# A graph-attention layer: gathers that skip the slots behind a group's last edge, with indices made by the vector engine

## The reference, cut to what matters

```python
q = (x @ Wq.T + bq); k = (x @ Wk.T + bk); v = (x @ Wv.T + bv)      # per node, 8 heads of 32
e = edge_attr @ We.T                                                # per edge, 64 -> 256
alpha = sum(q[dst] * (k[src] + e), axis=-1) / sqrt(32)
alpha = softmax of alpha over the edges with the same dst
out   = segment_sum((v[src] + e) * alpha, dst)
```

## Time and profile before

| | before |
|---|---|
| time, median of 2 runs | 5584.19 us (5583.86 to 5584.52) |
| profiled execution, first to last instruction | 5584.0 us |
| TensorE matmuls busy | 5115.2 us, 92% |
| GpSimd busy | 1895.7 us, 34% |
| mean granted TensorE clock | 0.907 of full |

### The profile page before, as it was taken

The page is one execution under the profiler, slowest core; times in us unless marked ns, Lnnn a source line. Parts: engine busy times, 40 slices in busy tenths (PEclk is TensorE's granted clock), DMA queues, the critical chain, the costliest instruction groups (busy, mean ns, idle before and its releaser), DMA issues. The chain is left out here.

```text
span 5584.0 us, 76757 instructions
## 1 busy us (share of the span) xinstructions
PE 5115.2 (92%) x22479; PEld 3611.0 (65%) x22479; DVE 1934.3 (35%) x4447; ACT 2257.3 (40%) x4140; POOL 1895.7 (34%) x2013
## 2 busy tenths in 40 slices
PE   4899999999999999999999999999999677877778
PEld 2577777777777777777777677777776454544545
DVE  3233233233333333333333332322333445445454
ACT  2344444444444444444444444444444323233233
POOL 1444444444444444444444444444443000000000
PEclk9899999999999999999999999999999877788778
DMA  2333333333333333333333433433433100000000
GB/s 102 94 103 96 96 100 98 97 98 94 102 96 96 103 95 95 102 92 95 103 95 95 105 94 92 104 93 96 103 94 86 61 13 20 13 13 20 13 13 7
DMA packets 486457, 445.39 MB, mean 80 GB/s; under 512 B 359613, under 2 KB 389310, under 8 KB 486408
## 3 DMA queue, kind: packets, MB, share of 16 engines
q0 software_dynamic: 96384, 265.00, 17.4%
q1 hardware_dynamic: 390024, 179.92, 12.8%
HBM read 431.89 MB, written 12.82 MB: 80 GB/s over the span
## 5 line engine op out<-in xcount | busy, mean ns | idle before, releaser
L494 POOL DMA_INDIRECT F<-xn_rows,srci x1970 | 1865.8, 947 | 2283.6 <-PE pZ L763 1799.4
L622 ACT ACTIVATE FT<-ring 128x256 f32<-128x256 f32 x1970 | 1196.9, 653 | 2328.9 <-PE ring L691 2327.2
L763 PE MATMUL pZ<-F,PT 128*128 128x321 f32 x3920 | 1380.7, 434 | 0.0
L699 PE MATMUL pS<-FT,G 128*128 128x320 f32 x3144 | 1096.0, 474 | 78.0 <-ACT FT L622 77.6
L699 PEld LDWEIGHTS pS<-FT,G 128*128 128x128 f32 x3144 | 613.0, 205 | 371.4 <-issue 202.2
L546 DVE COPY PT<-pPT 128x384 f32<-128x384 f32 (+1 forms) x786 | 348.8, 485 | 1327.8 <-PE pPT L706 1327.8
L691 PEld LDWEIGHTS ring<-ident,F 128*128 128x128 f32 x3940 | 481.5, 141 | 493.8 <-ACT FT L622 221.9
L691 PE MATMUL ring<-ident,F 128*128 128x128 f32 x3940 | 775.7, 282 | 7.4 <-DMA F<-xn_rows,srci 6.3
L763 PEld LDWEIGHTS pZ<-F,PT 128*128 128x128 f32 x3920 | 668.5, 191 | 105.0 <-issue 1.6
L539 DVE TENSOR_REDUCE nmx<-pS 128x1 f32<-128x640 f32 x393 | 324.0, 824 | 940.0 <-PE pS L699 935.3
L699 PE MATMUL pS<-F,G 81*128 81x320 f32 x1572 | 585.0, 454 | 0.0
(11 more groups left out here) (180 smaller groups left out, 3975.2 us busy)
## 6 DMA issues: line engine op xcount, KB each, us to landing
F<-in_edge_attrT SPq DMA_DIRECT2D x394, 160.0 KB
F<-in_edge_attr SPq DMA_DIRECT2D x394, 160.0 KB, 3.8
F<-xn_rows,srci POOLq DMA_INDIRECT x1970, 2.8
F<-in_dst SPq DMA_DIRECT2D x394, 42.5 KB
srci<-in_src SPq DMA_DIRECT2D x395, 2.5 KB, 3.3
x_all<-in_x SPq DMA_DIRECT2D x1, 6272.0 KB, 22.1
xn_rows<-xs SPq DMA_DIRECT2D x7, 896.0 KB, 3.9
xnb<-xn_rows SPq DMA_DIRECT2D x7, 896.0 KB, 4.8
```

Source lines behind the costliest of these rows:

```text
L494: pool.indirect_dma_start(out=F[s][:, t, 0:D], out_offset=None, in_=xn_d, in_offset=bass.IndirectOffsetOnAxis(ap=srci[j % GB][:, t:t + 1], ...
L622: act.activation(dst, src, ACT.Copy).then_inc(ring_emptied, 1)
L699: m = pe.matmul(pS[:, q, 0:SH], G[0:(P if k < KD else K3), k, j, :], f, start=(k == 0), stop=(k == 2))
L763: z = pe.matmul(pZ[:, 0:ZW], PT[:, t, :], F[s][:, t, 0:ZW], start=(t == 0), stop=(t == T - 1))
```

## The change

The source index of a slot whose destination lies at or behind the group's end is raised by 2^20, and the gather gets a bound of NP - 1 with out-of-range rows skipped. For this SyncE loads the destinations a second time, in the layout of the indices (`dsti`), and VectorE makes the indices (`gidx`) with two small operations on 128x5 at the head of each step, before `neq`. GpSimd waits for `gidx_ready` instead of the landed indices. The four F tiles are cleared once at the start of the stage, and two `iota`s fill `gend`, the ends of the groups.

```diff
+                            sp.dma_start(dsti[j % GB][:, :], a["dst"][bass.ds(o, CH)].rearrange("(p t) -> p t", t=T)
                                          ).then_inc(idx_landed[j % GB], 16)
...
                                 pool.indirect_dma_start(
                                     out=F[s][:, t, 0:D], out_offset=None, in_=xn_d,
-                                    in_offset=bass.IndirectOffsetOnAxis(ap=srci[j % GB][:, t:t + 1], axis=0),
+                                    in_offset=bass.IndirectOffsetOnAxis(ap=gidx[j % GB][:, t:t + 1], axis=0),
+                                    bounds_check=NP - 1, oob_is_err=False,
                                 ).then_inc(gathered[s], 16)
...
                         for j in range(2):
-                            pool.wait_ge(idx_landed[j], 16)
+                            pool.wait_ge(gidx_ready, j + 2)
                             gather(j)
...
                                     pool.wait_ge(slot_free, it * GB + (j + 3))
                                     pool.sem_inc(gather_turns, 1)
-                                    first = 1 if j + 2 < GB else 2
-                                    pool.wait_ge(idx_landed[(j + 2) % GB], it * 16 + 16 * first)
+                                    pool.wait_ge(gidx_ready, it * GB + (j + 4))
                                     pool.sem_inc(gather_turns, 1)
                                     gather(j + 2)
...
                         for s in range(SLOTS):
+                            ch.step(dve.memset(F[s][:, :, :], 0.0))
                             dve.memset(F[s][:, :, ONE:ONE + 1], 1.0).then_inc(slot_free, 1)
...
+                        def indices(j, c, landed, n):
+                            dve.wait_ge(idx_landed[j], landed)
+                            dve.wait_ge(gidx_ready, n)
+                            dve.tensor_scalar(past[:, :], dsti[j][:, :], gend[:, c], float(1 << 20),
+                                              ALU.is_ge, ALU.mult).then_inc(past_done, 1)
+                            dve.wait_ge(past_done, n)
+                            dve.tensor_tensor(gidx[j][:, :], srci[j][:, :], past[:, :], ALU.add).then_inc(gidx_ready, 1)
...
+                        dve.sem_inc(gidx_ready, 1)
+                        for j in range(2):
+                            indices(j, slice(j, j + 1), 32, j + 1)
...
                                 for j in range(GB):
+                                    indices((j + 2) % GB, bass.ds(b * GB + (j + 2), 1), it * 32 + 32 * (1 if j + 2 < GB else 2),
+                                            it * GB + (j + 3))
                                     neq((j + 2) % SLOTS, bass.ds(b * GB + (j + 2), 1), it * (32 * GB // SLOTS) + 32 * ((j + 2) // SLOTS + 1))
```

More of the change, by code:

```diff
@@ L305, in build @@
                 srci = [sbt(s2, f"srci{i}", [P, T], I32) for i in range(GB)]
+                dsti = [sbt(s2, f"dsti{i}", [P, T], I32) for i in range(GB)]
+                gidx = [sbt(s2, f"gidx{i}", [P, T], I32) for i in range(GB)]
+                past = sbt(s2, "past", [P, T])
+                gend = sbt(s2, "gend", [P, NG + 2])
                 FT = [sbt(s2, f"FT{i}", [P, KD, CH]) for i in range(2)]
@@ L375, in build @@
                 neq_done, pass_ready, qh_ready = sem("neq_done"), sem("pass_ready"), sem("qh_ready")
+                gidx_ready, past_done = sem("gidx_ready"), sem("past_done")
                 ring_filled, ring_emptied = sem("ring_filled"), sem("ring_emptied")
@@ L384, in build @@
                 NW2, NWV = 2, KD + 3
-                CONSTS2 = 15 + H
+                CONSTS2 = 17 + H
                 def long_loop(eng):
@@ L397, in load_indices @@
                             sp.dma_start(srci[j % GB][:, :], a["src"][bass.ds(o, CH)].rearrange("(p t) -> p t", t=T)
+                                         ).then_inc(idx_landed[j % GB], 16)
+                            sp.dma_start(dsti[j % GB][:, :], a["dst"][bass.ds(o, CH)].rearrange("(p t) -> p t", t=T)
                                          ).then_inc(idx_landed[j % GB], 16)
@@ L424, in _ @@
                         load_indices(at[2], 2)
-                        sp.wait_ge(consts2, 2)
+                        sp.wait_ge(consts2, 4)
                         for k in range(KD):
@@ L446, in _ @@
                                     load_indices(at[j + 1], j + 3)
-                            sp.wait_ge(idx_landed[2], (ps * NB + (NB + 1)) * 16)
+                            sp.wait_ge(idx_landed[2], (ps * NB + (NB + 1)) * 32)
                             sp.sem_inc(load_turns, 1)
@@ L454, in _ @@
                                   allow_small_or_imprecise_dtypes=True).then_inc(consts2, 1)
+                        pool.iota(gend[:, 0:NG], pattern=[[GN, NG]], base=GN, channel_multiplier=0,
+                                  allow_small_or_imprecise_dtypes=True).then_inc(consts2, 1)
+                        pool.iota(gend[:, NG:NG + 2], pattern=[[GN, 2]], base=GN, channel_multiplier=0,
+                                  allow_small_or_imprecise_dtypes=True).then_inc(consts2, 1)
                         pool.memset(WvT[:, :, :, :], 0.0).then_inc(consts2, 1)
@@ L458, in _ @@
                         pool.memset(selh[:, :], 1.0).then_inc(consts2, 1)
-                        pool.wait_ge(consts2, 5)
+                        pool.wait_ge(consts2, 7)
                         pool.iota(nid[:, NG:NG + 2], pattern=[[GN, 2]], base=-(DE + 1), channel_multiplier=1,
                                   allow_small_or_imprecise_dtypes=True).then_inc(consts2, 1)
-                        pool.wait_ge(consts2, 6)
+                        pool.wait_ge(consts2, 8)
                         pool.memset(nid[DE:DE + 1, :], -1.0e6).then_inc(consts2, 1)
-                        pool.wait_ge(consts2, 7)
+                        pool.wait_ge(consts2, 9)
                         g3 = G[:, KD, :, :].rearrange("p g (h n) -> p (g h) n", n=GN)
@@ L473, in _ @@
                                                base=-GN * h, pattern=[[-1, GN]], channel_multiplier=1).then_inc(consts2, 1)
-                            pool.wait_ge(consts2, 9 + h)
+                            pool.wait_ge(consts2, 11 + h)
                         pool.affine_select(out=selh[:, :], in_=selh[:, :], compare_op=ALU.is_ge, fill=0.0,
                                            base=0, pattern=[[-GN, H]], channel_multiplier=1).then_inc(consts2, 1)
-                        pool.wait_ge(consts2, 9 + H)
+                        pool.wait_ge(consts2, 11 + H)
                         pool.affine_select(out=selh[:, :], in_=selh[:, :], compare_op=ALU.is_ge, fill=0.0,
@@ L480, in _ @@
                         pool.memset(hmask[:, :], 1.0).then_inc(consts2, 1)
-                        pool.wait_ge(consts2, 11 + H)
+                        pool.wait_ge(consts2, 13 + H)
                         pool.affine_select(out=hmask[:, :], in_=hmask[:, :], compare_op=ALU.is_ge, fill=0.0,
                                            base=0, pattern=[[-C, HR]], channel_multiplier=1).then_inc(consts2, 1)
-                        pool.wait_ge(consts2, 12 + H)
+                        pool.wait_ge(consts2, 14 + H)
                         pool.affine_select(out=hmask[:, :], in_=hmask[:, :], compare_op=ALU.is_ge, fill=0.0,
                                            base=C - 1, pattern=[[C, HR]], channel_multiplier=-1).then_inc(consts2, 1)
-                        pool.wait_ge(consts2, 13 + H)
+                        pool.wait_ge(consts2, 15 + H)
                         pool.sem_inc(consts2, 2)
```

## The result

| | before | changed |
|---|---|---|
| time, median of 2 runs | 5584.19 us | 8640.85 us (8640.80 to 8640.91) |
| ratio to before | | 1.548 (95% interval 1.543 to 1.552) |

The change makes the kernel slower by more than half, 3057 us. The forecast was 8700 us in a range from 7800 to 9300.

What follows compares the result with a forecast made beforehand. The edge loop was taken as bound by TensorE; each block gains 7 x (5.9 + 2.2) + (4.3 + 2.2) = 63.2 us, so 5584 + 3097 + 8 = 8689, stated as 8700 us, range 7800 to 9300.

Steps and rivals of the forecast that it cites:

- What bounds the kernel, and where the new wait stands: Edge loop bound by TensorE; GpSimd's new wait stands behind VectorE's copies of the previous step, stopping TensorE 5.9 us a step.
- The path of the new wait: From VectorE's mask to TensorE's transposes: indices 0.38, GpSimd's start 0.75, five issues 5.01, landing and start 3.0 us.
- The first step of a block: At a block's first step, where VectorE reaches its mask after the merge, TensorE's pause is 4.3 us.
- The clock: TensorE restarts at the low clock after each pause, costing 2.2 us a step, with bounds of 0 and 3.1.
- What a gather costs: GpSimd's issue of a gather with bound and skipped rows stays at the 947 ns median; no change charged.
- Beside VectorE: Gathers now start where VectorE masks destinations; nothing charged, since second gathers ran beside the mask before at a 947 ns median.
- The start: Clears of 6.4 us at the stage's start, with the first two index sets and iotas: 8 us charged once.
- The sum: Over the edge loop, 63.2 us a block and 3097 us for 49 blocks, plus 8 at the start: 8700 us.
- The rival without the clock's price: TensorE's pauses cost no clock: 2247 us of pauses plus 8 at the start, about 7840 us; chance 0.14.
- The covered wait: VectorE's mask to landed rows takes no longer than TensorE's 3.2 us to its transposes: 5592 us; chance 0.03.
- Dearer gathers: A bound makes GpSimd's issue dearer, 0.25 us a gather, 1.3 a step: 9210 us; chance 0.13 for 9200 and more.
- Cheaper gathers: Skipped rows make GpSimd's issue cheaper in proportion, 0.84 us a step: 8370 us; chance 0.08 for 7700 to 8300.

Runs made afterwards that it cites:

- The wait alone: Kernel before, plus only GpSimd's gather waiting for a count VectorE raises at the head of its step; no index operations, bound or skipping: 8266 us, ratio 1.482.
- the pause filled: Changed kernel plus 11 extra matmuls on TensorE between a step's first pZ and the wait for gathers: 7923 us, ratio 1.419.
- the kernels with and without the bound: Changed kernel with offset 2^20 made 0, so nothing is skipped; with the bound kept 8645 us (1.549), with it removed 8641 us (1.548).

## Why the prediction was right

- **What bounds the kernel, and where the new wait stands.** Right. The wait alone gives 88% of the loss, and the indices one step ahead give all of it back.
- **The path of the new wait.** Predicted from VectorE's readiness: 0.38 + 0.75 + 5.01 + 3.0 = 9.1 us. Measured in the step shown: 0.42 for the indices (4021.76 to 4022.18), 0.87 to the first issue (4023.05), 5.21 to the fifth (4028.26) and 2.82 to TensorE's restart (4031.08), 9.3 us. The bounds for GpSimd's start were 0.30 and 1.0, and it lay near the upper one. The pause predicted as 5.9 us runs from where the transposes would have begun, 0.55 us behind the start of the first pZ; TensorE's wait begins at that pZ's end, 0.70 us behind its start. So the 5.85 of the step shown are 6.0 us on the prediction's measure.
- **The first step of a block.** Predicted 4.3 us, measured 4.7 on average over the block starts between 1000 and 4000 us (4.59 in the one shown, at 4013.34), or 4.9 on the prediction's measure.
- **The clock.** The mechanism was right and the size a little too large: 2.2 us a step predicted, 1.8 measured with the pause filled. A restart was expected at the low level for about 5 us; in the window above it lasted 3.9, and 3.9 us at half speed cost about 2.0. The Trainium skill's rule (TensorE: Matmul & The Clock Gate, "HAM oscillation — how this bites in real kernels") is that matmuls which wait for a DMA in each tile restart slow in each tile. The traces agree: 0.50 behind the pause shown, a mean of 0.78 over the loop, and 0.96 in the window with the pause filled.
- **What a gather costs.** I took no change, between -0.17 and +0.25 us an issue. It was +0.055, from the bound; skipped rows save nothing of an issue, even when they are all of them. So one of the signs that I had named for being wrong, a changed duration of the issue, did come. By the sum it is worth 0.22 us a step, 86 us; between the kernels with and without the bound the time differs by 4 us. That the term of nothing did no harm is in part the luck of that give-back.
- **Beside VectorE.** The charge of nothing was right, but the reason given isn't what happened: in the change the mask has ended (4022.21 + 0.55 = 4022.76) before the first gather starts (4023.05), and between 1000 and 4000 us no gather ran beside a mask. The two do run together in the kernel with the wait alone, where both start at 4008.08: there each group's first gather takes 958 ns on average and the four behind it 950, and the mask has a median of 545 ns, where the kernel before has 544. The Trainium skill's rule on the shared ports (SBUF — State Buffer, "Who interferes with whom") has one of the two blocked until the other is through, if the mask takes both ports; the most that the traces show of it here is that hundredth of a us.
- **The start.** 8 us charged; the kernel with the indices ahead has all of the start's work and is 4 us over the kernel before, within the noise, so 8 us is neither confirmed nor excluded.
- **The sum.** The pauses were put at 2247 us and the clock at 49 x 8 x 2.2 = 862. Measured: 7923 - 5584 = 2339 for all but the clock, with the start in it, and 718 for the clock. The two errors, +92 and -144, partly cancel, which is luck of sizes and not of the mechanism, and the forecast of 8700 is 59 us over the result. The blocks are 146.8 us apart where 148 was predicted, the ordinary steps 17.2 where it was 17.4, and the clock in the loop is 0.78 where it was 0.75. ScalarE's longest wait isn't for the DMA of F, as I had written, but for TensorE's transposes behind it (4970.1 us on the page). The rival without the clock's price, 7840, is within 83 us of the kernel in which that price was taken away.
- **The rivals.** The covered wait needs a path of 3.2 us against the 9.3 measured. Dearer gathers: the bound's 0.055 us an issue is a fifth of the bound of 0.25 that was priced. Cheaper gathers: excluded by the kernel that skips everything.

## What to carry to other kernels

A wait on an engine that works in order takes over everything that stands ahead of the signal in that engine's queue. Before adding one, find when that engine reaches the place, compare it with the reserve of the transfer that it releases, and, if it is too late, make the value one step earlier: here that cost nothing and took back 3057 us. Work that is taken out of a transfer nobody waits for brings no time. And a pause in each step of a TensorE loop can be paid twice, once as idle time and once at the low clock behind it: here that was so with 5.7 us of pause and for the most part with 2.8, and no longer with 1.1.

## What the runs showed of the hardware that I had not expected

- An indirect gather with a bound takes GpSimd 998 to 1002 ns to issue instead of 946 to 949, whether no row, 17.8% or all rows are skipped. The gather queue shows 96384 packets in each case, with 265.00, 218.17 and 7.80 MB. The totals fit a skipped row that still moves 4 bytes.
- With nothing to move, it still took 2.2 us from the last issue of a group to TensorE's restart, against 2.8 with the rows.
- A time saved in the pause was lost to a longer low-clock stretch behind it in one pair of kernels: 5.64 against 5.83 us of wait, 7.56 against 7.17 us of restart, and the same total of 8641 and 8645 us. What sets this isn't known from these runs.
- A bare count in VectorE's queue seems to be raised before the copy ahead of it has ended: GpSimd's gather and VectorE's mask both began at 4008.08, 0.03 us after that copy, where GpSimd took 0.87 us from the end of an index operation that carried the count.
